# Rounding the attention weights one slot earlier on ScalarE

## The reference

```python
x = x + tanh(g_xattn[0]) * attn(_layernorm(x), ctx, ctx, mask, Wq, Wk, Wv, Wo)
x = x + tanh(g_ffn[0]) * ffn(_layernorm(x), gate_*, up_*, down_*)

# attn: 32 query heads, 8 heads of K and V, 128 wide
q = apply_rope((query @ Wq).reshape(b, t, 32, 128))
k = apply_rope((key @ Wk).reshape(b, t, 8, 128))
v = (value @ Wv).reshape(b, t, 8, 128)
logits = 30 * tanh(einsum(q, k) * 0.0883 / 30)
logits = where(mask, logits, -1e30)
weights = softmax(logits)                      # "p" below, not yet divided by its sum
attn = einsum(weights, v).reshape(b, t, 4096) @ Wo

# ffn: Wg, Wu, Wd unpacked from int4 with scales and zeros
out = (silu(x @ Wg) * (x @ Wu)) @ Wd
```

## Time and profile before

| | |
|---|---|
| timed runs of before | 771.16 us median of 3 (771.05 to 772.77) |
| the profiled execution | 773.69 us, span 771.9 us |
| busy in the span | PE 731.7 us (95%), PEld 607.0 (79%), DVE 607.2 (79%), POOL 500.7 (65%), ACT 426.2 (55%) |
| mean granted TensorE clock | 0.973 |

### The profile page before, as it was taken

The page is one execution under the profiler, slowest core; times in us unless marked ns, Lnnn a source line. Parts: engine busy times, 40 slices in busy tenths (PEclk is TensorE's granted clock), DMA queues, the critical chain, the costliest instruction groups (busy, mean ns, idle before and its releaser), DMA issues. The chain is left out here.

```text
span 771.9 us, 11046 instructions
## 1 busy us (share of the span) xinstructions
PE 731.7 (95%) x3394; PEld 607.0 (79%) x3394; DVE 607.2 (79%) x931; ACT 426.2 (55%) x770; POOL 500.7 (65%) x379
## 2 busy tenths in 40 slices
PE   3989999999999999999999999999779789999998
PEld 3868888888888888888888888888557578888786
DVE  6688888878888887988888788888997578778521
ACT  4676666665666666566666656664443345555420
POOL 5576877777687777758777775876583376656400
PEclk9899999999999999999999999999888799999999
DMA  9321013000201300020120003003220234442011
GB/s 276 100 83 42 1 42 96 14 1 28 96 1 41 96 15 0 28 96 1 42 95 15 1 28 96 0 1 82 49 65 0 66 90 95 116 98 41 0 69 41
DMA packets 70621, 41.53 MB, mean 54 GB/s; under 512 B 23242, under 2 KB 63050, under 8 KB 70570
## 3 DMA queue, kind: packets, MB, share of 16 engines
q1 hardware_dynamic: 70570, 40.90, 18.8%
HBM read 38.77 MB, written 2.11 MB: 53 GB/s over the span
## 5 line engine op out<-in xcount | busy, mean ns | idle before, releaser
L581 POOL TENSOR_TENSOR aT_lo<-attn,aT_hi 128x512 fp32r<-128x512 f32 x64 | 83.1, 1299 | 96.0 <-ACT aT_hi L792 96.0
L55 PE MATMUL ps_o<-wo_hi,aT_hi 128*128 128x512 f32 x256 | 102.6, 401 | 0.5 <-DVE acc L1135 0.5
L55 PE MATMUL bank_q<-xT_hi,wq_hi 128*128 128x512 f32 x256 | 101.0, 394 | 1.7 <-DVE qT_lo L946 1.7
L57 PE MATMUL ps_o<-wo_hi,aT_lo 128*128 128x512 f32 x256 | 101.0, 395 | 0.0
L56 PE MATMUL ps_o<-wo_lo,aT_hi 128*128 128x512 f32 x256 | 100.8, 394 | 0.0
L56 PE MATMUL bank_q<-xT_lo,wq_hi 128*128 128x512 f32 x256 | 100.7, 393 | 0.0
L57 PE MATMUL bank_q<-xT_hi,wq_lo 128*128 128x512 f32 x256 | 100.5, 393 | 0.0
L673 ACT CAST qT_hi<-bank_q 128x512 fp32r<-128x512 f32 x64 | 37.6, 587 | 112.7 <-DVE bank_q L940 112.7
L509 POOL TENSOR_TENSOR q_sin<-q_sin,q_tab 128x512 f32<-128x512 f32 x64 | 83.3, 1301 | 19.7 <-ACT q_sin L666 18.0
L501 POOL TENSOR_TENSOR probs<-probs,keepT 128x512 f32<-128x512 f32 x64 | 83.2, 1300 | 11.5 <-ACT probs L802 11.5
L932 DVE TENSOR_TENSOR bank_q<-bank_q,q_tab 128x512 f32<-128x512 f32 x64 | 44.7, 699 | 34.6 <-ACT q_sin L666 34.6
(11 more groups left out here) (215 smaller groups left out, 2071.8 us busy)
## 6 DMA issues: line engine op xcount, KB each, us to landing
wq_raw<-in_Wq SPq DMA_DIRECT2D x32, 256.0 KB, 2.8
wo_raw<-in_Wo SPq DMA_DIRECT2D x8, 1024.0 KB, 5.5
packed<-in_gate_q SPq DMA_DIRECT2D x40, 64.0 KB, 2.3
packed<-in_up_q SPq DMA_DIRECT2D x40, 64.0 KB, 2.3
packed<-in_down_q SPq DMA_DIRECT2D x10, 256.0 KB, 3.3
acc<-in_x SPq DMA_DIRECT2D x8, 256.0 KB, 5.5
cT_raw<-in_ctx SPq DMA_DIRECT2D x8, 256.0 KB, 5.9
wk_raw<-in_Wk SPq DMA_DIRECT2D x8, 256.0 KB, 2.7
```

The lines of the kernel that those rows point to most:

```text
L55: nc.tensor.matmul(out, w_hi, m_hi, start=first, stop=False)
L57: return nc.tensor.matmul(out, w_lo, m_hi, start=False, stop=last)
L581: nc.gpsimd.tensor_tensor(aT_lo[:], attn[:], aT_hi[:].bitcast(F32), ALU.subtract).then_inc(a_split, 1)
```

## The change

ScalarE rounds p of slot s within slot s, behind exp and ahead of the rounding of Q job s + 4, for s up to 56 (`P_EARLY` = 57). From s = 57 on, p is rounded first in the slot behind, as before. Nothing is added or removed, and the other engines' order is the same.

```diff
@@ -42,6 +42,7 @@
 TAIL = SLOTS - B
 AHEAD = HALF
 SHIFT = TAIL + 2
+P_EARLY = TAIL + 1
@@ -803,12 +804,10 @@
                 def slot(s):
-                    if runs(s - 1) and s > TAIL:
+                    if runs(s - 1) and s - 1 >= P_EARLY:
                         round_p(s - 1)
                     if runs(s - 2):
                         round_a(s - 2)
-                    if runs(s - 1) and s <= TAIL:
-                        round_p(s - 1)
                     for kind, g, part in parts_of(s):
                         if s != 0:
                             round_w(kind, g, part)
@@ -822,6 +821,8 @@
                         turn_k(kj)
                     if runs(s):
                         cap_and_exp(s)
+                        if s < P_EARLY:
+                            round_p(s)
                     for n in q_of(s):
                         round_q(n)
```

## The result

| | before | after |
|---|---|---|
| timed runs, median (range) | 771.88 us (770.24 to 773.74, 18 runs) | 773.39 us (771.81 to 775.23, 18 runs) |
| ratio, 95% interval | | 1.002 (1.0012 to 1.0027) |
| the same two kernels, second set of runs | 771.80 us (29 runs) | 772.75 us, ratio 1.0009 (1.0000 to 1.0017) |
| profiled execution, span | 773.69 us, 771.9 us | 772.65 us, 770.9 us |
| busy PE, DVE, ACT, POOL | 731.7, 607.2, 426.2, 500.7 us | 729.1, 621.2, 425.8, 498.6 us |

The change costs 1.5 us in the first set (0.9 to 2.1) and 0.7 us in the second (0 to 1.3). That is within the 0.3% that the prediction called no change, on the slow side of it.

A forecast was written before the change was run, and what follows sets the result against it. TensorE was taken as the bound, busy 485.74 of 486 us from 60 to 546 us. First slot +0.47 and slot 56 -0.26 gave +0.2 us, 771.16 to 771.4; range for 8 in 10: 770.2 to 773.8.

The forecast's parts named there:

- The full part: 60 to 546 us, TensorE busy 485.74 of 486: ScalarE changes worth nothing unless they remove two waits or make new ones.
- The first slot, +0.47: Slot 0: later wo rounding delays GpSimd's second weight split, then p_lo and the row sums' matmul, by 0.47 us.
- Slots 8, 24 and 40, cost 0: Slots with 0.35 to 0.36 us margin: aT_lo and p_lo 0.17 later in slot 8, covered by the margin; cost 0.
- R: The end of the rotary add on VectorE; in slot 8 at 115.90, with the mask's end at 115.56.
- rival 1: Slower: loop through the mask, 7.25 against 7.08 us; delay d costs 13 x (d - 0.5) + 3 x (d - 0.25); 775.3; 8%.
- the 13 others: Slots such as 7, 23, 39, 55 with 0.60 to 0.62 us margin: a delayed 0 to 0.3 us, no wait.
- Slot 56, -0.26: Last slot whose p moves: a starts 0.34 earlier, p_lo ends earlier, TensorE's row sums gain 0.26 us.
- A: Theory: loss in the first slot alone; for p rounded twice, a about 0.8 late, some 3.5 us, ratio 1.005 to 1.006.
- Rival 2: Faster: first slot's wait, up to 2.53 us, goes with the slow clock stretch behind it, 1.65 us; 767.0; 3%.
- Rival 3: First slot's stall, 3.0 instead of 2.5 us, lengthens the slow stretch; one more costs 1.65 us: 773.0; 10%.
- B: Theory of the experiments: the longer first wait costs clock behind it, beyond its 0.5 us.
- my own case: Whole kernel +0.2 us, with -0.3 to +1.0 around it: 770.9 to 772.2 us; 46%.

The follow-up runs named there:

- wo_idle: The changed kernel with the third part of the first output weights rounded on ScalarE in slot 0, between exp and p: 771.85 us, 1.0001 to before.
- plo_56: The kernel before with p early in slot 56 only, and VectorE taking p's rest of slot 0 ahead of Q's rest: 770.94 us, 0.9984.
- plo_first: The changed kernel with VectorE taking p's rest of slot 0 ahead of Q's rest in slot 1: 770.25 us, 0.9978 to before.
- p56_only: The kernel before with p rounded early in slot 56 alone: 770.98 us, 0.9984.
- p_twice: The changed kernel with p rounded twice in slots 1 to 56, the second rounding waiting for the first: 785.23 us, 1.0175 to before.

## Why the prediction was right, and where its sizes were off

- **The full part is worth nothing to this change: right.** p's rounding stands directly behind the mask, ScalarE waits there instead of for the add (from 60 to 546 us its waits ahead of Q's rounding fall from 104 to 4 us, and 93 us stand ahead of p's), and 60 to 546 us are as full as before.
- **The first slot, +0.47: right**, in place, mechanism and size (3.0 instead of 2.5 us). wo_idle takes it away by removing the one step named, ScalarE's later `wo` rounding. The collision it rests on held in every profile of slot 0 in which the split came first: `p_lo` ended 0.54 to 0.56 us behind it (among them after, wo_idle, plo_56), and took 0.68 where it came first itself (plo_first). The Trainium skill (SBUF — State Buffer, "Who interferes with whom") says that the instruction that issues first keeps the shared port; this trace agrees: plo_56 and plo_first show both outcomes for the same pair of instructions.
- **Slots 8, 24 and 40, cost 0: mis-sized.** I had slot 8's a's rest 0.17 us later, which the margin covers. It is 0.37 later against TensorE: from its start to the row sums it was 119.33 - 117.12 = 2.21 us and is 118.46 - 116.51 = 1.95, of which 0.11 is the wait. The step that failed is that the 0.17 left the mask of slot 8 where it was, 0.34 ahead of R; it is 0.20 ahead now (114.78 against R at 114.29 + 0.69 = 114.98). GpSimd's queue from slot 7's a's rest to that mask, before and after, shows why:

```profile
109.79 1.30 POOL L581 TENSOR_TENSOR aT_lo<-attn,aT_hi 128x512 fp32r<-128x512 f32 x1 [1.43 <-ACT aT_hi L792]
...
113.02 1.29 POOL L509 TENSOR_TENSOR q_sin<-q_sin,q_tab 128x512 f32<-128x512 f32 x1 [0.22 <-ACT q_sin L666]
```

```profile
109.28 1.29 POOL L582 TENSOR_TENSOR aT_lo<-attn,aT_hi 128x512 fp32r<-128x512 f32 x1 [1.74 <-ACT aT_hi L793]
...
112.22 1.30 POOL L510 TENSOR_TENSOR q_sin<-q_sin,q_tab 128x512 f32<-128x512 f32 x1
```

Before, the stretch took 114.26 - 109.79 = 4.47 us, 0.22 of it idle; after, 113.47 - 109.28 = 4.19 with no gap. Slot 7's a is 0.42 later against TensorE (2.04 us ahead of the row sums instead of 2.46); 0.28 of that is taken up here, and 0.14 reaches the next mask, the next p and the next a. That is the loop of rival 1. Slot 7's 0.42 has a turn of it in it already: its own mask is 0.10 ahead of R where it was 0.21, since slot 6's a is 0.17 later, so it lies above the 0.3 that I took as the most. I had the loop's length and its condition, and priced it only as a rival; this part of it belongs in the forecast. It costs 0.1 us in each of the three slots. Of the 13 others the four directly ahead of a slot of small margin (7, 23, 39, 55) went from 0.60 to 0.20; the other nine kept their 0.60 to 0.62, and no wait arose in any.
- **Slot 56, -0.26: -0.16**, for the same reason (its mask, too, is 0.19 ahead of R where it was 0.34); in p56_only, where the slots ahead keep the old order, all of it is gained.
- **Rival 1's price was too low.** p_twice shows the loop adding up where short slots follow each other. In slot 8 a's rest starts there 1.22 us ahead of the earliest start of the row sums (119.81 to 120.80 + 0.23), which is 0.99 later than before; for that delay in every slot the formula gives 13 x 0.49 + 3 x 0.74 = 8.6, and the trace has 11.5. And the delay itself was set too low in the expectation for A (0.8), since it grows where slots follow each other.
- **Rival 2** went wrong as a forecast, but its price was real: with VectorE's order changed too, the first wait shrinks and the slow stretch goes. **Rival 3** is B above.
- **The sum.** Forecast +0.2, trace +0.6, measured +1.5 (0.9 to 2.1) and +0.7 (0 to 1.3). The 0.4 between forecast and trace are the three slots and slot 56. The second measurement fits the trace. Between trace and the first one 0.9 us are open: outside the moved part the profiles of this kernel differ by more than that (from the start to the first scores 45.6 to 46.9 us in three), so a wait of that size could not be read there. The clock may be part of it: the mean granted clock of the changed kernel is 0.9777 in the first set and 0.9788 in the second, 0.8 us of the span apart; for the kernel before none is on record in the first set.
- **The range.** The median of 773.39 us lies within 770.2 to 773.8, but above my own case, 770.9 to 772.2. 0.7 us of that is the kernel before itself, 771.88 in this set where I started from 771.16. That it still fell inside is luck in part: the upper end was set for a second slow stretch (rival 3), and the runs don't show that as the cause.

## What to carry to other kernels

Moving a ready-to-run instruction forward on an in-order engine buys nothing while its consumer sits behind other work on its own engine; what it does is delay everything it was moved past. Follow each of those to its last user, and also once round the loop back to the instruction's own release: where that loop is as long as the period, small delays add up instead of vanishing. And look for the second edit, on the consumer's engine, without which the first is only a cost.

## What the runs showed of the hardware

- A VectorE subtraction of 128x512 that takes 0.68 us alone ended 0.54 to 0.56 us behind the GpSimd one that had started ahead of it, wherever that one held it up. In the changed kernel it so took 1.5 to 1.7 us in 30 of 58 slots; the 14 us of busy time that this added cost TensorE 0.3 us.
- Behind a TensorE wait of 1.5 us the granted clock stayed at 1.00 in four profiles of four; behind 2.5 us it was at 0.50 for part of the next 10 us in five of five; behind 3.0 us the outcome varied, in five, from none to twice that length.
- Shortening one wait by 1.0 us was worth 2.6 us up to the row sums of slot 1, since the whole stretch behind it ran at 2.4 GHz, where 3.41 us had been at 1.2.
